# A two-layer decoder's delta rule stage with its triangular systems stored mirrored, every solve operation placed singly, and the order of all five engines rewritten

## What is computed

```python
k = short_conv(x @ Wk.T + bk, wk_conv, bk_conv)      # 4 taps; q and v alike
beta = sigmoid(x @ Wbeta.T + bbeta)
v = silu(v);  k, v = k / (|k| + eps), v / (|k| + eps);  q = q / (|q| + eps)
def step(S, (q_t, k_t, v_t, b_t)):                    # per batch and head (16 heads of 32)
    pred = k_t @ S
    S = S + b_t * outer(k_t, v_t - pred)
    return S, q_t @ S
o = rmsnorm(scan(step), norm_w)
x = layernorm(x + o @ Wo.T + bo)
```

## Time and profile before

| | us |
|---|---|
| median of three runs | 2806.24 |
| the profiled execution, its own time | 2803.46 |
| its span, first to last instruction | 2801.7 |
| PE busy | 2551.3 (91%) |
| DVE busy | 2227.7 (80%) |
| ACT busy | 1416.5 (51%) |
| POOL busy | 511.3 (18%) |
| mean granted TensorE clock | 0.971 of full speed |

### The profile page before, as it was taken

How to read it: one execution, slowest core, us unless ns; L and a number is a source line. 1 busy time by engine, 2 the same in 40 slices (tenths; PEclk the granted TensorE clock), 3 DMA queues, 4 the chain that set the end, 5 groups by cost and what they waited for, 6 DMA issues and landing times. The chain is left out here.

```text
span 2801.7 us, 82999 instructions
## 1 busy us (share of the span) xinstructions
PE 2551.3 (91%) x35304; PEld 1802.2 (64%) x35304; DVE 2227.7 (80%) x4030; ACT 1416.5 (51%) x2566; POOL 511.3 (18%) x661
## 2 busy tenths in 40 slices
PE   7798889998989878999999997998889999999998
PEld 5666666666666656776776764344467777776665
DVE  3898998888999727888888784987878888883786
ACT  7667765677656322233333222544466666652454
POOL 2223322233222210000000000003711111110122
PEclk9899999999999988999999999999999999999999
DMA  2001111111111312212211112566951222214331
GB/s 89 18 19 34 53 37 34 41 34 34 56 34 43 129 43 81 68 54 70 66 54 61 61 55 96 186 216 217 336 176 46 86 66 61 90 49 155 99 125 72
DMA packets 165805, 234.24 MB, mean 84 GB/s; under 512 B 17858, under 2 KB 94018, under 8 KB 162884
## 3 DMA queue, kind: packets, MB, share of 16 engines
q1 hardware_dynamic: 165444, 229.01, 24.7%
HBM read 136.18 MB, written 92.80 MB: 82 GB/s over the span
## 5 line engine op out<-in xcount | busy, mean ns | idle before, releaser
L612 PE MATMUL delta_banks<-both_columns,both_mats 128*128 128x256 f32 x1536 | 387.9, 397 | 5.0 <-ACT both_line L865 3.4
L612 PEld LDWEIGHTS delta_banks<-both_columns,both_mats 128*128 128x128 f32 x1536 | 282.6, 193 | 49.4 <-ACT both_line L865 6.3
L883 ACT ACTIVATE both_product<-both_line,delta_conv_w 128x256 f32<-128x256 f32 x576 | 248.6, 496 | 6.8 <-DVE both_conv L1105 5.8
L1512 PE MATMUL ctxatt_banks<-both_product,ctxatt_oT 128*128 128x512 f32 x512 | 228.4, 599 | 4.9 <-DVE both_conv L1627 4.9
L1473 PE MATMUL ctxatt_banks<-both_line,both_mats 128*128 128x256 f32 x960 | 221.1, 384 | 1.4 <-SPq L1424 1.4
L1473 PEld LDWEIGHTS ctxatt_banks<-both_line,both_mats 128*128 128x128 f32 x960 | 180.4, 193 | 24.8 <-SPq L1424 1.7
L1162 DVE TENSOR_TENSOR delta_squares<-delta_t_sys 128x30 f32<-128x30 f32 (+14 forms) x480 | 176.2, 367 | 12.5 <-issue 0.2
L1165 DVE TENSOR_TENSOR delta_t_sys<-delta_t_sys,delta_squares 128x30 f32<-128x30 f32 (+14 forms) x480 | 165.5, 345 | 16.5
L865 ACT ACTIVATE both_line<-delta_banks,delta_proj_b 128x256 f32<-128x256 f32 x192 | 87.8, 458 | 175.9 <-PE delta_banks L612 175.7
L1512 PEld LDWEIGHTS ctxatt_banks<-both_product,ctxatt_oT 128*128 128x128 f32 x512 | 95.3, 191 | 115.5 <-issue 109.0
L1559 ACT ACTIVATE ctxatt_probsT<-ctxatt_banks 128x512 f32<-128x512 f32 x128 | 69.5, 594 | 189.2 <-PE ctxatt_banks L1494 189.2
(11 more groups left out here) (367 smaller groups left out, 5810.9 us busy)
## 6 DMA issues: line engine op xcount, KB each, us to landing
h<-ffn_hid SPq DMA_DIRECT2D x66, 256.0 KB, 2.1
xT<-both_newT SPq DMA_DIRECT2D x24, 512.0 KB, 3.6
x<-both_new SPq DMA_DIRECT2D x24, 512.0 KB, 4.0
x<-decay_last SPq DMA_DIRECT2D x24, 512.0 KB, 7.4
ffn_hid<-h SPq DMA_DIRECT2D x6, 1536.0 KB, 7.9
both_columns<-xT SPq DMA_DIRECT2D x16, 512.0 KB, 4.7
delta_x<-x SPq DMA_DIRECT2D x16, 512.0 KB, 4.0
both_line<-xT SPq DMA_DIRECT2D x16, 512.0 KB, 4.8
```

Of the source, the lines that this page charges most:

```text
L612: mm = pe.matmul(b_proj[:, p % 2, 0:B * P], wT[NAMES[i]][:, k, g * P:(g + 1) * P], xT_sb[:, n.parity, k], start=k == 0, stop=k == KB - 1)
L883: made = act.activation(slot(n, i)[:, j - 1, g].rearrange("p (b t) -> p b t", b=B), line[:, i, g, :, j:j + P], ACT.Copy, scale=conv_w[:, i ...
L1512: mm = pe.matmul(b_o[:], oT[:, b, k, :], wo[:, k, :], start=k == 0, stop=k == PAIRS - 1)
```

## The change

Only `delta_rule_attention` changes. The helpers:

```diff
-        masked_kq = sb("masked_kq", [P, 2, ITEMS, 2, DD])
+        masked_kq = sb("masked_kq", [P, 3, ITEMS, DD])
         t_sys = sb("t_sys", [P, DD, DD])
+        t_raw = sb("t_raw", [P, DD, ITEMS])
...
                 def copy_history(n, i):
                     if not isinstance(n.index, int) or n.index > 0:
                         wait(pool, taps_made, n, TAP_OPS, (i + 1) * KB - TAP_OPS)
+                        wait(pool, first_made, n, TAP_OPS, (i + 1) * KB - TAP_OPS)
...
                 def scale_t(n):
                     wait(pool, solved, n, SOLVE_OPS, SOLVE_OPS)
-                    pool.tensor_tensor(tT[:], tT[:], rate_of(n), ALU.mult).then_inc(t_scaled, 1)
+                    wait(pool, updated, n, CHUNKS, 0)
+                    pool.tensor_tensor(tT[:], t_raw[:].rearrange("p t i -> p i t"), rate_of(n), ALU.mult).then_inc(t_scaled, 1)
...
                 def square(n, i):
                     wait(act, turned[i], n, 1, 1)
                     if i == 0:
                         wait(act, ss_made, n, SS_OPS, 1 - SS_OPS)
-                        wait(act, solved, n, SOLVE_OPS, 0)
...
-                    dve.tensor_tensor(masked_kq[:, n.parity, rows], products, weights_kq[:, rows], ALU.mult).then_inc(masked, 1)
+                    of_keys_and_queries = masked_kq[:, 0:2 + n.parity:1 + n.parity, rows].rearrange("p a i t -> p i a t")
+                    dve.tensor_tensor(of_keys_and_queries, products, weights_kq[:, rows], ALU.mult).then_inc(masked, 1)
 
                 def to_systems(n):
...
-                    dve.transpose(t_sys[:].rearrange("p i j -> p j i"), masked_kq[:, n.parity, :, 0].rearrange("p i s -> p s i")).then_inc(systems, 1)
+                    dve.transpose(t_sys[:], masked_kq[:, 0].rearrange("p i s -> p s i")).then_inc(systems, 1)
...
                 def substitute(n, k):
...
+                    if k == 0:
+                        wait(dve, t_scaled, n, 1, 0)
                     j = k // 2 + 1
                     rows = DD - 1 - j
-                    parts, to = flat(squares[:, 0])[:, 0:rows * j].rearrange("p (i c) -> p i c", i=rows), t_sys[:, j + 1:, 0:j]
+                    parts, to = flat(t_raw[:])[:, 0:rows * j].rearrange("p (c i) -> p c i", c=j), t_sys[:, 0:j, j + 1:]
                     if k % 2 == 0:
-                        c.did(dve.tensor_tensor(parts, t_sys[:, j + 1:, j:j + 1].to_broadcast([P, rows, j]),
-                                                t_sys[:, j:j + 1, 0:j].to_broadcast([P, rows, j]), ALU.mult))
+                        c.did(dve.tensor_tensor(parts, t_sys[:, 0:j, j:j + 1].to_broadcast([P, j, rows]),
+                                                t_sys[:, j:j + 1, j + 1:].to_broadcast([P, j, rows]), ALU.mult))
...
-                    wait(dve, updated, n, CHUNKS, 0)
-                    c.did(dve.transpose(tT[:].rearrange("p i t -> p t i"), t_sys[:]))
+                    c.did(dve.transpose(t_raw[:], t_sys[:].rearrange("p j i -> p i j")))
```

All lists `step(n)` are rewritten, with a fifth tile back (`t5`), so 21 steps in place of 20. `solve(n, q)`, a packet of four substitutions, is gone; each `substitute(n, k)` stands alone. On DVE the step's border moves: `mask`, `to_systems` and substitutions 0 to 11 of a tile now stand at the end of the step before. POOL's and SP's lists:

```diff
@@ POOL
+                    if t4:
+                        add_bias(t4)
+                    if t1:
+                        copy_history(t1, 2)
                     if t2:
                         rate_keys(t2)
                         mask_beta(t2)
                         pair_taps(t2, 2)
+                    if t4:
+                        scale_outputs(t4)
                     if t1:
                         pair_taps(t1, 0)
-                        copy_history(t1, 2)
                     if n:
                         copy_history(n, 0)
-                    if t4:
-                        scale_outputs(t4)
...
-                    if t3:
-                        add_bias(t3)
@@ SP
+                    if n.index == STEPS + 1:
+                        load_keys()
+                    if t5:
+                        store(t5)
                     if n:
                         load_columns(n)
...
-                    if t4:
-                        store(t4)
```

444 lines of the change are left out of this document (247 added, 197 removed).

## The result

| | before | after |
|---|---|---|
| median, us (4 runs each, same chip) | 2805.54 | 2771.84 |
| lowest and highest | 2800.96, 2809.28 | 2763.09, 2775.90 |
| ratio after / before, 95% interval | | 0.9872 [0.9855, 0.9890] |
| the profiled execution, its span | 2801.7 | 2773.5 |
| mean granted TensorE clock | 0.971 | 0.972 |

The change is faster by 33.7 us. The forecast of 2763 us was right in its direction, and the time lies in its range, but 43 us of gain were laid and the interval of the ratio gives only 31 to 41. The profiled execution of after, at 2775.3 us, is one of the slower of its four.

The account below looks back on a forecast made before the run. No engine bounds alone: PE waits mostly for DVE, DVE for POOL. DVE's terms sum to -3.75 us, PE and jitter make 55.7 us a tile for 58.96; with the stage's ends 43.0 us less, 2763 us, range 2740 to 2797.

Parts of the forecast that it names:

- the two collisions: DVE operations standing still during POOL's second and third `pair_taps`; removing them was laid at -1.5 and -0.4 us a tile.
- Term 1: On DVE, `rms_invert` no longer meets POOL's second `pair_taps`: -1.5 us a tile.
- term 4: On DVE, the other `join` no longer waits for its pair, as `rms_invert` stands ahead: -0.65 us a tile.
- Term 2: POOL's third `pair_taps` partly dodges DVE's substitutions, falling on `add` and `turn` of v: -0.4 us a tile.
- term 5: On DVE, more work between T and `carry` 0 covers the wait for `step_state`: -0.5 us a tile.
- term 3: On DVE, a `join` moved away no longer covers the wait for POOL's weights: +1.0 us a tile.
- term 7: DVE's transposes `to_systems` and `from_systems` fall to 1.48 us each with a strided read: -1.1 us a tile.
- term 6: DVE waits less at `add`, where PE comes late to `project_out` after a lower clock: -0.6 us a tile.
- some 1.5 us of true issue gaps: PE's idle time per tile without a wait for another engine, added to its 51.75 us at full clock.
- Rival C: Slower: PE gets ahead, stands at `predict` 2 and 3, and its clock falls; 2837 us, chance 9%.
- rival A: DVE stays the bound, third `pair_taps` still hits, transposes give only 0.24: 57.6 us a tile, 2788 us, chance 23%.
- 0: ACT's `square` loses its wait for the solve: On ACT, removing this wait was laid at 0, since ACT has a third of its time free.

Follow-up runs that it names:

- experiment 4: The kernel before with one swap in DVE's list, `rms_invert` ahead of the `join` of slot 2: 2785.31 us, ratio 0.9928.
- experiment 5: The changed kernel with ACT's `gate` moved back behind the last q taps: 2782.40 us, ratio 0.9913.
- experiment 12: The changed kernel with `project` 9 ahead of `outputs` 0, `carry` 1 and 2 earlier, and the slot 2 `join` back behind `invert_norms`: 2764.85 us, ratio 0.9863.
- experiment 3: The changed kernel with one wait put back, ACT's `square` waiting for the solve of the tile before: 2783.36 us, ratio 0.9925.
- experiment 8: The changed kernel with `project` 9 moved on PE to between `update` 2 and `outputs` 0: 2767.69 us, ratio 0.9855.

## Why the prediction was right or wrong

**Right: the two collisions.** Term 1, laid at -1.5, is -1.77 by the record (2.10 to 0.33), and experiment 4 has it together with term 4 at 1.78 us a tile, of 2.4 that DVE saves. Term 2, laid at -0.4, is larger: nine hits of 2.0 became one of 2.0 and three of 0.85, so 1.5 a tile became 0.4, -1.1; experiment 5 puts 0.89 of it back by one move in ACT's list. The near thing fell to the good side, which is in part luck: the third `pair_taps` comes 29.1 us after T's end (348.60 less 319.52), somewhat ahead of the 29.7 to 30.8 laid, and DVE is just at `add`.

**Right: terms 4 and 5.** The waits of `join` (7.7 us in 12 tiles) and of `carry` 0 (6.3) are gone.

**Wrong: term 3**, the wait for POOL's weights. Laid as 1.92 to 2.9, it went to 20.2 / 12 = 1.7. The step that failed is "the weights come 3.3 us after the inversion" taken as fixed. They come 2.3 us after it now (from 327.92 to 330.26), since `rate_keys` had been held by the very join that was thought to cover the wait; experiment 12 shows it held and not held. The prediction had read that a DVE operation with two SBUF inputs stands still for POOL. It had not asked for the same the other way round, though the earlier trace rows hold two records of one shape at 2.36 and 2.50 us, and the trace of before has `rate_keys` at 1.12 us for 32 elements.

**Wrong: term 7**, the transposes, laid at -1.1 from 2.16 and 1.92 to 1.48. They came to 1.98 and 1.96, so -0.14. The step that failed is the choice of the value: a strided read was priced by what it adds to a strided write, 0.24. But beside a strided write most of the read's cost is hidden, and on its own it costs 0.72, about what the write costs (0.68). The Trainium skill's rule (SBUF — State Buffer, "Door 1: The DMA port swizzle", on cachelines) has a cost for a stride beyond 4 fp32 elements and makes no difference between reading and writing; by it the prediction had a one-sided 1.92 and a term of -0.24. Here the trace bears it out: 1.96 to 1.98 for the read alone, 1.92 for the write alone. POOL pays too: `scale_t` with its strided read takes 2.51 us in the mean for 1.93. No engine's list of waits names it.

**Wrong: term 6** and what it stood on, "most falls of the clock go". The waits at `add` went from 11.6 to 16.6 us, the granted clock of the steady part stayed at 0.98, with nine falls for six. The old gap ahead of `project_out` 1 is indeed gone (PE waits for no `add` any more), but supply gaps of 1 to 2.8 us, most of them inside `outputs`, took its place, and beside them the clock fell, and then DVE waits for `project_out` 0, for `turn` of k's buffer and at `miss`. Together DVE's waits are 64.6 us in the 12 tiles, 51.2 before.

**Wrong: a term of PE's sum**, "some 1.5 us of true issue gaps". By the packets the supply gaps were 28.2 / 12 = 2.35 us a tile already before, and after they are 40.1 / 12 = 3.34, which is 1.8 more than laid. The rest of the sum is near: PE is busy 52.57 for 51.75, 0.8 more, the falls of the clock among it. The wait before `predict` 2 comes twelve times, 0.8 to 1.6 us, 1.0 in the mean for the 0.9 laid. The 1.1 laid before `predict` 3 is there in two tiles only, since PE comes late, so the waits for `carry` are 1.3 where 2.0 were laid. With the 0.4 added for jitter that is 1.8 + 0.8 - 0.7 - 0.4 = 1.5 of the 1.6 us by which the period misses the forecast. Rival C had the right kind of chain, a gap that moves and takes the clock along, but at the wrong place and at too high a price.

**Nearer to rival A by the period.** 57.27 us lies beside A's 57.6 and not beside 55.7. Of A's four conditions two came true: the transposes gave no more than its 0.24, and term 6 gave nothing. The other two did not, since the third `pair_taps` seldom hits and term 5 gave its 0.5. Nor did DVE stay the one bound: it now waits for PE, and PE for its instructions.

**The ends of the stage.** Filling was costed at 0 and gave 5.3 us; the 13th tile and the drain were laid at 1.6 + 2.4 and gave -2.6 + 3.5. With 39.0 laid for the 12 tiles and 20.3 found, the 5.3 of the filling hid a part of the error, and so did 5 us more between the medians than between the profiled executions. That the time came out within 9 us of the forecast, when the steady part gave half of what was laid, is in part luck.

**"0: ACT's `square` loses its wait for the solve"** is the largest of the terms costed at nothing: experiment 3 gives it 11 us, or 15 by the ratios.

**Shown and not shown.** That PE stands in `outputs` for want of instructions is shown by the traces: 304 of its 305 gaps there, over all 14, end 1.15 to 1.65 us after an instruction packet has landed. That a dense order makes them is borne out twice. In the 2 us ahead of its 31 supply gaps of 0.95 us or more the changed kernel has a median of 240 records of PE, against 116 in any 2 us; and `outputs` has 256 records in 1.3 us, as many as a packet brings, while no two packets of the stage start less than 3.2 us apart in any trace. And experiment 8 lowered the gaps in `outputs` by PE's order. What sets the start of a packet, which in the worst gap came only when PE had nothing left to begin, stays open. So does why the tiles from 391 to 687 us take 59.1 us in the mean in the changed kernel and the others 55.9; in the kernel before it was 59.3 and 58.7.
